# Gated cross-attention block on one core: another order of the beginning, eight score products between two bank pairs, and reciprocals by turned blocks

## The reference

```python
x = x + tanh(g_xattn) * xattn(layernorm(x), ctx)     # x 4 x 2048 x 512, ctx 4 x 154 x 512
x = x + tanh(g_ffn)   * ffn(layernorm(x))
xattn: q = x Wq + bq; k, v = ctx Wkv + bkv           # 16 heads of 32
       softmax(q k / sqrt(32)) v, then Wo, bo
ffn:   relu(x w1 + b1) -> fp8 (e4m3); w2 -> fp8; product + b2, rounded to fp16
```

## Time and profile before

| | |
|---|---|
| median of 3 runs | 1587.6 us (1587.31 to 1588.94) |
| profiled execution | 1588.39 us, of which the traced span is 1586.6 us |
| PE busy | 1533.4 us, 97% of the span |
| DVE, POOL, ACT busy | 60%, 55%, 51% |
| TensorE clock granted, mean | 0.988 |

### The profile page before, as it was taken

The page is one execution under the profiler, slowest core; times in us unless marked ns, Lnnn a source line. Parts: engine busy times, 40 slices in busy tenths (PEclk is TensorE's granted clock), DMA queues, the critical chain, the costliest instruction groups (busy, mean ns, idle before and its releaser), DMA issues.

```text
span 1586.6 us, 23629 instructions
## 1 busy us (share of the span) xinstructions
PE 1533.4 (97%) x8600; PEld 695.7 (44%) x8600; DVE 951.8 (60%) x1297; ACT 813.5 (51%) x1196; POOL 877.2 (55%) x919
## 2 busy tenths in 40 slices
PE   7776999999999999999999999999999999999998
PEld 4322444444444444444444444444444444444443
DVE  7768665665746566574746657574665757445231
ACT  3674664645555464555546454545545455455421
POOL 3679465564746555574646547464654746445310
PEclk9988999999999999999999999999999999999999
DMA  8355464454544354354445434344543434333120
GB/s 338 94 152 150 128 157 122 134 116 112 109 139 94 117 136 113 101 114 138 104 119 132 115 103 119 115 103 131 135 114 104 120 113 104 100 100 86 44 54 27
DMA packets 252855, 186.70 MB, mean 118 GB/s; under 512 B 160012, under 2 KB 209476, under 8 KB 251076
## 3 DMA queue, kind: packets, MB, share of 16 engines
q1 hardware_dynamic: 252740, 185.19, 43.9%
HBM read 99.95 MB, written 51.59 MB: 96 GB/s over the span
## 4 chain that ended last, share of the span: by engine, by line
PE 73%; DVE 11%; POOL 7%; issue 4%; ACT 2%; DMA 2%; SPq 1%; DVEq 0%; ACTq 0%
PE ring L519 52%; PE ring L728 8%; PE m_ps L621 4%; DVE y L1035 3%; PE s_ps L651 2%; PE y_ps L679 2%; DVE bns L1060 2%; DVE resid L1077 2%; POOL pmain L1144 2%; POOL rs L1182 2%; DVE xn L1086 1%; PE d_ps L668 1%; POOL x L1170 1%; PE s_ps L644 1%; DMA yT<-in_wq_t 1%
## 5 line engine op out<-in xcount | busy, mean ns | idle before, releaser
L519 PE MATMUL ring<-late_a,w 128*128 128x512 f16 (+1 forms) x3096 | 703.1, 378 | 1.5 <-DMA late_a<-x 1.5
L519 PEld LDWEIGHTS ring<-late_a,w 128*128 128x128 f16 x3096 | 301.9, 98 | 338.8 <-issue 8.6
L1144 POOL TENSOR_TENSOR pmain<-p,pmain 128x512 f16<-128x512 f32 x256 | 304.3, 1191 | 173.8 <-ACT p L814 170.6
L836 ACT ACTIVATE late_b<-ring,b_sb,wsc 128x512 fp8e4<-128x512 f32 x256 | 199.3, 779 | 388.1 <-PE ring L519 388.1
L1013 DVE TENSOR_REDUCE smax<-m_ps 128x4 f32<-128x616 f32 x256 | 203.4, 794 | 229.6 <-PE m_ps L621 229.2
L1035 DVE RECIPROCAL y<-d_ps 128x256 f32<-128x256 f32 x128 | 223.4, 1745 | 58.6 <-PE d_ps L671 57.1
L814 ACT ACTIVATE p<-s_ps,prob_log,sc 128x512 f32<-128x512 f32 x320 | 247.9, 775 | 0.1
L728 PE MATMUL ring<-w,late_b 128*128 128x512 fp8e4 x1024 | 228.5, 379 | 5.4 <-DVE ffn L1044 3.8
L811 ACT ACTIVATE pmain<-s_ps,prob_log,sc 128x512 f16<-128x512 f32 x256 | 198.1, 774 | 2.7 <-PE s_ps L651 2.7
L1144 POOL TENSOR_TENSOR pleft<-p,pleft 128x512 f16<-128x512 f32 x64 | 76.9, 1201 | 183.3 <-ACT p L814 183.3
L519 PE MATMUL ring<-wo,yT 128*128 128x512 f16 x768 | 175.2, 382 | 0.0
(11 more groups left out here) (149 smaller groups left out, 1424.0 us busy)
## 6 DMA issues: line engine op xcount, KB each, us to landing
qstack<-q_rows SPq DMA_DIRECT2D x192, 128.0 KB, 3.1
pstack<-left_rows SPq DMA_DIRECT2D x192, 128.0 KB, 2.6
xin<-in_x SPq DMA_DIRECT2D x64, 256.0 KB, 3.1
q_rows<-qparts SPq DMA_DIRECT2D x32, 512.0 KB, 2.8
left_rows<-pleft SPq DMA_DIRECT2D x64, 256.0 KB, 2.5
resid<-in_x SPq DMA_DIRECT2D x64, 256.0 KB, 3.0
out_x<-resid SPq DMA_DIRECT2D x64, 256.0 KB, 2.7
resid<-in_w_t SPq DMA_DIRECT2D x5, 1024.0 KB, 5.5
```

Source lines behind the costliest of these rows:

```text
L519: last = pe.matmul(dst, lhs(a, k), rhs(b, k), start=(k == 0 and p == 0), stop=(k == n_k - 1 and p == 2))
L836: nc.scalar.activation(hT[:, j, :], ring_bank("h", c, j)[:], ACT.Relu, bias=b1_sb[:, j:j + 1], scale=wsc[:, j // 4, 1:2], saturate=False). ...
L1144: nc.gpsimd.tensor_tensor(part[:, 1, :], p32[:, n % 2, :], part[:, 0, :], ALU.subtract).then_inc(prob_lo, 1)
```

## The change

It touches three things. Names and numbers of beats are as above.

**1. Order and scales of the beginning.** `FIRST` is -14 for -12. Ahead of the loop stand only key jobs 0 and 1, then query jobs 0 and 1; key jobs 2 and 3 move into the loop (`KV_STEPS`), and `first_blocks` is split by pairs and between DVE (two heads) and ACT (two heads). The values get a scale of their own: wv leaves the first fold and enters the second (`magnitudes(5)` on ACT), and `o_w1_scales` moves from beat 1 to beat -6. On SP wv is issued after wq, biases and gates. All tables of chunks 0 to 2 have new numbers.

```diff
-            for n in range(KT):
+            for n in range(2):
                 keys_values(n)
             query_out(0, 0)
-            first_blocks()
+            first_blocks(0)
             query_out(0, 1)
...
-W_FOLD = {0: 1}
+W_FOLD = {0: -6}
...
+            def moved(dst, src):
+                return nc.vector.tensor_reduce(dst, src.unsqueeze(2), AX.X, ALU.max)
...
-                dve.wait_ge(summed, 5)
+                dve.wait_ge(summed, 6)
```

```diff
+PAIRED = {(0, 1), (0, 3), (0, 5), (0, 7)}
...
-                if c + u:
+                if (c, u) == (0, 0):
+                    pe.wait_ge(turn_moved, TILES)
+                elif (c, u) == (0, 1):
+                    pe.wait_ge(q_moved, 2)
+                elif (c, u - 1) in PAIRED or (c, u) in PAIRED:
+                    pe.wait_ge(maxed, c * 16 + u - 1)
+                else:
                     pe.wait_ge(maxed, c * 16 + u)
```

```diff
-            def normalise(c, k):
-                nc.vector.reciprocal(y32[:, cols], d_ps[:, cols]).then_inc(inverted, 1)
-                dve.wait_ge(inverted, 2 * g + half + 1)
-                dve.wait_ge(valued, g + 1)
-                nc.vector.tensor_tensor(y32[:, cols], y_ps[:, cols], y32[:, cols], ALU.mult).then_inc(y_scaled, 1)
+            def normalise(c, m):
+                nc.vector.transpose(y32[:], d_ps[:]).then_inc(den_turned, 1)
+                dve.wait_ge(den_turned, g + 1)
+                nc.vector.reciprocal(inv[:], y32[:].rearrange("p (b j) -> p b j", j=DH)[:, :, 0]).then_inc(inverted, 1)
+                dve.wait_ge(inverted, g + 1)
+                nc.vector.transpose(y32[:], inv[:].unsqueeze(2).to_broadcast([P, CHUNK // DH, DH])).then_inc(spread, 1)
+                dve.wait_ge(spread, g + 1)
+                dve.wait_ge(valued, g + 1)
+                nc.vector.tensor_tensor(y32[:], y_ps[:], y32[:], ALU.mult).then_inc(y_scaled, 1)
...
-O_AT = [33, 34, 35, 36]
+O_AT = [32, 33, 34, 35]
```

More of the change, by code:

```diff
@@ L35 @@
 W_LOG = 13
+V_LOG = 14
 PERIOD = 28
@@ new lines @@
+BLOCKS_AT = {1: -8}
+QUERY_ROWS_AT = {1: -4}
+VALUE_ROWS_AT = {0: 3}
+KSTACK_AT = {0: -13, 1: -5, 2: -5, 3: -5, 4: 0, 5: 0, 6: 4, 7: 6}
+KEYS_OUT_AT = {0: 31}
+GATE_AT = {0: -7}
+BIAS_AT = {0: -6}
+W1_SUM = {0: -12, 1: -12, 2: -11, 3: -6}
+WQ_HI = {0: 3}
+WQ_LO = {0: 5}
+W_FOLD = {0: -6}
+WO_HI = {0: -5}
+WO_LO = {0: 15}
+W1_HI = {0: 13, 1: 22, 2: 23, 3: 27}
+W1_LO = {0: 13, 1: 23, 2: 41, 3: 41}
+W2_LOAD = {0: 21, 1: 43, 2: 49, 3: 49}
+PAIRED = {(0, 1), (0, 3), (0, 5), (0, 7)}
+W2_PART = {0: 42, 1: 45, 2: 46, 3: 50}
@@ L490, in _ @@
             for beat in range(FIRST, (NCH - 1) * PERIOD + LAST):
-                if beat == KV_STEPS[4][3]:
-                    values_stacked(0, 0)
-                    q_out(0, 1)
-                    q_in(0, 1)
+                once(lambda pair: q_out(0, pair), QUERY_ROWS_AT, beat)
+                once(lambda pair: q_in(0, pair), QUERY_ROWS_AT, beat)
+                once(lambda b: values_stacked(b, 0), VALUE_ROWS_AT, beat)
                 run(lambda c, t: x_load(c, t) if c > 1 else None, XLOAD_AT, beat)
@@ L791, in stack_keys, with first_blocks @@
                                stack_bank[n % 2][0:96, 0:HK].rearrange("p (h k) -> p h k", h=2)).then_inc(kcat_set, 1)
+            def first_blocks(pair):
+                act.wait_ge(kv_hi, 2 * pair + 2)
+                for h in range(2, GH):
+                    nc.scalar.copy(kblk[DH * h:DH * h + DH, 2 * pair:2 * pair + 2, h * NK:(h + 1) * NK],
+                                   kst[DH * h:DH * h + DH, 0, 2 * pair:2 * pair + 2, 0:NK]).then_inc(kblk_set[pair], 1)
             def gate(n):
@@ L862, in y_hi @@
             def y_hi(c, m):
-                act.wait_ge(y_scaled, 2 * group(c, m) + 2)
+                act.wait_ge(y_scaled, group(c, m) + 1)
                 if m == 0 and c:
@@ L876, in _ @@
             act.wait_ge(cleared, 1)
+            magnitudes(5)
             magnitudes(4)
-            magnitudes(0)
-            for n in range(KT):
+            for n in range(2):
                 keys_values(n)
-            for m in range(2):
-                query_hi(0, m)
+            query_hi(0, 0)
+            first_blocks(0)
+            query_hi(0, 1)
             for beat in range(FIRST, (NCH - 1) * PERIOD + LAST):
@@ L891, in _ @@
                 run(lambda c, t: x_hi(c, t) if c else None, XSPLIT_AT, beat, XSPLIT_OWN)
+                once(first_blocks, BLOCKS_AT, beat)
                 once(stack_keys, KSTACK_AT, beat)
@@ L1102, in _ @@
                     ln1_apply(0, t - 1)
-            for n, (name, src) in ((1, ("ctx", ctx_raw)), (2, ("wk", wk_raw)), (3, ("wv", wv_raw)), (0, ("wq", wq_raw))):
+            for n, (name, src) in ((1, ("ctx", ctx_raw)), (2, ("wk", wk_raw)), (0, ("wq", wq_raw))):
                 dve.wait_ge(w_in[name], DMA)
@@ L1118, in _ @@
                 run(shift, SHIFT_AT, beat, SHIFT_OWN)
-                run(normalise, NORMAL_AT, beat)
                 run(ln2_apply, LN2_AT, beat, LN2_OWN)
+                once(o_w1_scales, W_FOLD, beat)
+                once(value_bias, BIAS_AT, beat)
                 steps_of(KV_STEPS, lambda n, k: keys_values(n) if k == KT - 1 else None, beat)
@@ L1123, in _ @@
                 run(residual, O_AT, beat, O_OWN)
+                run(normalise, NORMAL_AT, beat)
                 run(finish, FFN_AT, beat, FFN_OWN)
```

178 lines of the change are left out of this document (86 added, 92 removed).

## The result

The changed kernel takes **1570.4 us** (median of 4 runs, 1569.2 to 1575.8) beside 1587.5 us for the kernel before (1587.3 to 1588.9): ratio 0.990, 95% interval 0.9886 to 0.9912. The forecast was 1570 us, with a range of 1560 to 1581. The total is as forecast; parts that it was added up from are not, and their errors cancel, as the traces and twelve runs show.

A forecast was written before the change was run, and what follows sets the result against it. PE's fixed work bounds the kernel, plus about 47 us it loses in the beginning, mostly behind DVE. Gains 4 + 4 + 7 + 6 - 3 = 18 us off the profiled 1588.4 gave 1570.4, median 1570 us, range 1560 to 1581.

The forecast's parts named there:

- signs of being wrong: Middle chunk off 92.1 us; turns over 1 us; first `value` not before 70, or SP idle; `row_max` waits unchanged.
- Cost of the new `normalise`: DVE, per head group: two turns of 0.71, reciprocal 0.18, product 0.69, gaps 0.1; 2.4 us, 2.0 less than before.
- It gives nothing in the middle, because PE hides it: Middle chunks: DVE saves 8 of 57 us per chunk, but no time is gained, since only PE's own work counts.
- covered by 1.8 and 3.8 us: Middle chunks: `y_lo` ends before the earlier `project`, by 1.8 us without the shorter `normalise` and 3.8 with it.
- Rival C: Dear turns, decided above 2.6 us each: at 3.5 us `project` stalls 1.7 us per middle chunk, 1610 us; chance 0.05.
- Start to the first `value`, gain 4: First 70 us: earlier scales and ranks, SP setting the end; first `value` at 67 instead of 70, gain 4 us.
- under 2 us: Stage from 20 to 52 us: worth of the paired banks alone, counted within the start's gain of 4.
- 70 to 122 us, gain 4: Three head groups cost DVE 2.0 us less each, where 14.2 us are lost; POOL lets only 4 us through.
- rival A: Beginning: POOL and SP take over from DVE as the limit, gain only 7.5 us, total 1580 us; chance 0.24.
- 122 to 170 us, gains 7 and 6: 122 to 140: two more `project` jobs and a shorter chain, 7; 140 to 170: `normalise`, low part, query job, 6.
- B: Beginning packs better: first `value` at 63, stages to 158 lose a third; gain 26 to 30, 1560 us; chance 0.14.
- D: New holes, a longer one before the second fold, eat the gain: 2 or 3 us left, 1585 us; chance 0.10.

The follow-up runs named there:

- turned_behind: Kernel before with only the turned-reciprocal `normalise`, its issuing line moved behind `residual`: 1587.6 us, ratio 1.0001.
- beat_earlier: Kernel before with the new `normalise` behind `residual`, plus the changed kernel's middle tables one beat earlier and its `HIDDEN_HALVES`: 1583.8 us, ratio 0.9974.
- turned_only: Kernel before with only the reciprocals of `normalise` replaced by turns, all at the beat of its first half: 1598.3 us, ratio 1.0062.
- turns_twice: Changed kernel with each of the two turns of `normalise` issued twice: 1589.0 us, ratio 1.0007 to the kernel before.
- rows_between: Changed kernel with SP's queue reordered: `vstack` loads between `q_out` and `q_in`, chunk 1's first transpose behind `left_rows`: 1567.7 us, ratio 0.9882 to the kernel before.
- two_beats: Changed kernel with the old reciprocals in two halves at two beats, splitting of y one beat later: 1588.3 us, ratio 1.0002 to the kernel before.
- plain_recip: Changed kernel with the old reciprocals, both halves at the beat of the new `normalise`: 1599.3 us, ratio 1.0066 to the kernel before.
- second profile: Profiled execution from running the changed kernel again, nothing altered; that run's median was 1571.4 us, ratio 0.9886 to the kernel before.

## Why the total was right and the parts were not

The total came out by luck, as the sum below shows. Two of the forecast's own signs of being wrong came true: a middle chunk off 92.1 us, and, from 70 to 122 us, waits for `row_max` as long as before.

**Cost of the new `normalise`: right.** Turn 0.707 and 0.711 us (forecast 0.71), short reciprocal 0.25 (0.18), product 0.69 (0.69), together 2.4 us.

**"It gives nothing in the middle, because PE hides it": the step that failed.** The forecast read 91.8 of 92.1 us busy as full and asked only whether `y_lo` ends before `project`. The middle gives 5.6 us and the end 1.4, with the tables that no longer let `finish` stand behind a late product (turned_behind against beat_earlier). And what was called covered by 1.8 and 3.8 us isn't: the bounds are `residual` behind `normalise` on DVE (turned_only, +0.86 a chunk) and the exponentials behind `y_hi` on ACT (turns_twice, +1.15). Rival C's point of decision, 2.6 us a turn, is far too high: with a room of 0.5 us PE begins to wait at some 1.0 us a turn (an estimate, 0.71 + 0.5 / 2), and at 1.42 the whole gain was gone.

**Start to the first `value`, gain 4: right, with its reasons.** 3.4 to 3.6 us. `left_rows` at 59.5 (60), `value` at 66.5 (67), the fold at 43 to 46.6 us (42 to 46), small reductions 0.14 to 0.19 us, the hole behind the fourth query's move 1.8 us at 47 (2 at 46). The first `rank` came at 28.1 instead of 27: it waits 2 us for the two blocks of keys that ACT now copies. SP as the bound was shown by rows_between. The pairs, "under 2 us", are worth 3 to 4 by the medians.

**70 to 122 us, gain 4: failed.** PE's waits for `row_max` halved over the whole beginning (25.5 to 12.9 us), but ahead of 70 us and behind 122: in this stage they are 6.9 us and were 7.3. First to fourth `value` takes 52.6 us beside 52.2, and the loss by the windows is 15.9 us beside 14.2. With two_beats and plain_recip the fourth `value` comes 3 to 4 us later, so the turns do save their part here, and the new order spends as much. The timeline names two places. PE waits 2.2 us at 88 for DVE to move a value job out (L1030), which it didn't before. And the longest wait for `row_max` is 3.4 us, where the whole `normalise` (from 101.30 us on) and a layer norm's product of 1.40 us stand ahead of it on DVE. PE, then DVE:

```profile
105.93 0.42 PE L638 MATMUL m_ps<-kblk,qparts 128*128 128x308 f16 x2 [3.40 <-DVE smax L1048]
103.68 1.40 DVE L1107 TENSOR_SCALAR xin<-xin,mv,rs 128x512 f32<-128x512 f32 x1
```

It looks like turned_only's case, but no run moves `normalise` in this stage alone, so what the stage lost by stays open. POOL is busy for 32.7 of the 40 us from 82, and was for 30.7. The stage's gain went as in rival A; that POOL or SP took over is not shown.

**122 to 170 us, gains 7 and 6: part of it.** By the windows the two stretches from 122 to 158 and the one to 170 lose 14.5 us beside 21.0 (11.4 in the second profile): 6.5 and 9.6 us less, and 13 were forecast. The first `value` of chunk 1 came at 137.6 and 139.2, not near 130, the first `hidden` at 148.7 and 151.6, not near 139.

**Sum.** Forecast 21 - 3 in the beginning and 0 later; measured 10.3 (second profile), 5.6 and 1.4. The 18 us came out since an error of -7.7 in the beginning met one of +7 in the middle and at the end, which the forecast had put at nothing: that is luck. Rivals B, C and D can be dropped; A's loss of the gain held in one stage.

**What the change is made of.** Turned reciprocals behind `residual`: 1587.6. With the middle tables too: 1583.8. The whole new order with the old reciprocals: 1588.3. All together: 1570.4. Neither the turns alone nor the order alone is worth anything. The short `normalise` gives ACT and DVE room, and only the tables turn that room into less waiting.

## What to carry to other kernels

Where each engine runs a fixed order, ask of a shorter instruction not how busy its engine is, but which instruction behind it another engine waits for, and what stands in that other engine's queue behind the wait; read the waits of the steady state to the last 0.3 us, since it is paid in every chunk. Test a step's room by doubling it: the distance to its nominal consumer (3.8 us here) was not the room (0.5). And change the order and the cost together: the two halves of such a change, measured apart, can each show nothing or a loss.

## What the hardware showed beyond that

**A turn costs the same from PSUM and from SBUF**, 0.707 and 0.711 us on 128x512, though the second reads 16 columns stretched to 512. The Trainium skill, "VectorE: DVE Perf Modes", section on the TRN2 errata, has 58 cycles + columns for a source in SBUF, by which I had put the second turn at 0.59 as an estimate; the trace doesn't bear that out. The same section's figure for an fp32 addition, columns + 151 cycles at 0.96 GHz, gives 0.69, which is the product's 0.691 and close to the turns.

**The layer norm's product takes 0.55 us, and 1.37 where POOL starts just ahead of it**, and a turn isn't touched. From 690 us in the changed kernel, DVE and POOL:

```profile
690.56 1.37 DVE L1123 TENSOR_SCALAR xn<-resid,mv,rs 128x512 f32<-128x512 f32 x1 [1.23 <-POOL rs L1220]
693.45 0.70 DVE L1068 STREAM_TRANSPOSE y<-d_ps 128x512 f32<-128x512 f32 x1
```

```profile
690.49 1.16 POOL L1203 TENSOR_TENSOR x<-xin,x 128x512 f16<-128x512 f32 x1
692.91 1.15 POOL L1208 TENSOR_TENSOR x<-xn,x 128x512 f16<-128x512 f32 x1
```

POOL's instruction started 0.07 us ahead of DVE's product, and the product ended 0.28 us after it (691.93 beside 691.65). At 695.83 POOL's instruction had 0.27 us left to run, and the product took 0.55. This agrees with the rule of "SBUF — State Buffer", section "Who interferes with whom" in the Trainium skill, by which whoever issues first holds the shared ports and the other waits; that the product waited for these ports is the page's explanation, and the trace shows only the times.

**PE's clock differs between two executions of one kernel.** In the first profile of the changed kernel PE was busy for 0.56 of the 4 us ahead of 156, its clock fell within them, and it had the lower of its two levels (1.2 GHz) in the 4 us behind; in the second, whose clock had been lower between 144 and 152 us (0.87 and 0.70 in the two windows of 4 us), it had been busy for 2.95 and had the upper (2.4 GHz) on both sides of 156. Windows of PE alone, first profile and then second:

```profile
152.00:156.00 4.00, 0.56 (x3) 0.77 0.33 72
156.00:160.00 4.00, 4.00 (x21) 0.50 0.04 6
```

```profile
152.00:156.00 4.00, 2.95 (x28) 1.00 0.31 68
156.00:160.00 4.00, 4.00 (x30) 1.00 0.04 6
```

The same 36 matmuls of `hidden` took 8.08 us in the one and 5.37 in the other. They began at the same time, 155.44 and 155.40 us: PE waited 3 us longer for x2 in the first profile (3.96 beside 1.05), but in the second it had come to them as much later. So 2.7 of the 4.6 us between the two executions are the lower clock in these 36. Most of the rest is a wait of 1.67 us, 24 us further on, which the second profile doesn't have. PE waits for ACT there, and ACT had waited for the load of a part of w2:

```profile
187.31 2.76 PE L532 MATMUL ring<-late_a,w 128*128 128x512 f16 x12 [1.67 <-ACT late_b L859]
```
